# Row vectors turned on TensorE instead of through DRAM, lane sums on VectorE, low parts on GpSimd

## The reference

```python
xn = _layernorm(x, axis=-1)
x = x + attn(xn, ...) + ffn(xn, ...)
# attn
q, gate, k, v = split(xn @ w_qkv.T)            # 16, 16, 4, 4 heads of 128
q, k = _rope(_layernorm(q, ...)), _rope(_layernorm(k, ...))
scores = einsum('bhqd,bhkd->bhqk', q, k) / math.sqrt(D)
scores = where(causal, scores, -inf)
out = einsum('bhqk,bhkd->bhqd', softmax(scores), v)
out = (out * sigmoid(gate)) @ w_o.T
# ffn
top_vals, top_idx = top_k(xn @ w_router, 2);  probs = softmax(top_vals)
y = square(relu(xn @ w_fc[e])) @ w_proj[e]     # of a token's two experts, weighted by probs
```

## Time and profile before

| what | value |
|---|---|
| median of 3 runs (lowest to highest) | 2317.14 us (2312.96 to 2319.57) |
| the profiled execution, its own time | 2312.64 us |
| its span, first to last instruction | 2310.8 us |
| mean granted TensorE clock | 0.853 of full speed |
| busy: PE, DVE, ACT, POOL | 71%, 70%, 54%, 55% |
| bytes moved | 112.09 MB, 49 GB/s in the mean |

### The profile page before, as it was taken

One profiled execution on the slowest core, in us unless ns is written; L12 is line 12 of the kernel. 1 busy time (PEld: TensorE's weight loads), 2 busy tenths in 40 slices (PEclk: granted clock), 3 DMA queues, 4 the chain that ended last, 5 costly groups with the idle time before them and its releaser, 6 DMA issues.

```text
span 2310.8 us, 24049 instructions
## 1 busy us (share of the span) xinstructions
PE 1635.4 (71%) x7139; PEld 1284.1 (56%) x7139; DVE 1625.4 (70%) x2926; ACT 1242.2 (54%) x2409; POOL 1272.1 (55%) x1113
## 2 busy tenths in 40 slices
PE   5676676767767777777765767668767568678676
PEld 3455555555546565655644655556545456566564
DVE  7776677776766666877755666677856558688784
ACT  3445455556545555656644545556654346566565
POOL 6655667775644544555643544545555335556464
PEclk8887788878878888898897888889887879898888
DMA  4312311222342122122113212202212132321101
GB/s 164 97 40 29 48 29 37 49 49 55 46 53 51 35 51 48 28 60 56 48 37 58 51 23 58 44 21 67 47 46 53 37 49 44 69 39 33 37 10 46
DMA packets 130451, 112.09 MB, mean 49 GB/s; under 512 B 73872, under 2 KB 99984, under 8 KB 130128
## 3 DMA queue, kind: packets, MB, share of 16 engines
q1 hardware_dynamic: 126576, 100.29, 21.1%
q0 software_dynamic: 3744, 10.26, 1.6%
HBM read 91.61 MB, written 24.98 MB: 50 GB/s over the span
## 4 chain that ended last, share of the span: by engine, by line
DMA 29%; DVE 10%; PE 5%; issue 3%; POOL 2%; ACT 2%; SPq 0%; POOLq 0%; DVEq 0%; ACTq 0%
DMA inv_of<-row_inv 10%; DMA min_of<-row_min 8%; DMA min_rows<-min_of 4%; DMA inv_rows<-inv_of 3%; DVE pT_lo L1350 2%; PE st_bank L1437 2%; DMA expert_raw<-in_w_proj 2%; DVE t_same L1305 1%; DVE chunk_min L1338 1%; PE bank L1437 1%; DMA y_of<-rows,row_to 1%; POOL lane_sum L942 1%; DVE bank L1335 1%; POOL oT L949 1%; ACT st_bank L1069 1%
## 5 line engine op out<-in xcount | busy, mean ns | idle before, releaser
L942 POOL TENSOR_TENSOR lane_sum<-lane_sum,pT_raw 128x512 f32<-128x512 f32 x420 | 600.7, 1430 | 202.3 <-ACT pT_raw L1079 177.3
L1350 DVE TENSOR_TENSOR pT_lo<-pT_raw,pT_hi 128x512 fp32r<-128x512 f32 x544 | 502.4, 933 | 152.9 <-ACT pT_hi L1086 151.6
L1437 PE MATMUL st_bank<-qT_hi,kT_hi 128*128 128x512 f32 x544 | 262.8, 483 | 341.6 <-ACT st_bank L1069 341.0
L1069 ACT ACTIVATE st_bank<-min_rows 128x512 f32<-128x512 f32 x480 | 284.4, 596 | 322.5 <-DMA min_rows<-min_of 316.4
L1079 ACT ACTIVATE pT_raw<-st_bank 128x512 f32<-128x512 f32 x544 | 322.8, 594 | 191.3 <-PE st_bank L1437 76.7
L1086 ACT ACTIVATE pT_hi<-pT_raw 128x512 fp32r<-128x512 f32 x544 | 338.3, 627 | 60.4 <-PE o_bank L1437 53.6
L1437 PEld LDWEIGHTS st_bank<-qT_hi,kT_hi 128*128 128x128 f32 x544 | 118.2, 217 | 403.4 <-ACT st_bank L1069 388.1
L1437 PE MATMUL o_bank<-pT_hi,v_hi 128*128 128x512 f32 x544 | 240.5, 442 | 65.7 <-DVE pT_lo L1350 57.7
L1338 DVE TENSOR_REDUCE chunk_min<-bank 128x1 f32<-128x512 f32 (+1 forms) x384 | 242.1, 648 | 30.8 <-PE bank L1515 30.5
L949 POOL TENSOR_TENSOR oT<-oT,inv_rows 128x512 f32<-128x512 f32 x63 | 82.9, 1316 | 289.1 <-DMA inv_rows<-inv_of 288.2
L1437 PE MATMUL st_bank<-qT_lo,kT_hi 128*128 128x512 f32 x544 | 241.2, 443 | 0.0
(11 more groups left out here) (176 smaller groups left out, 3779.4 us busy)
## 6 DMA issues: line engine op xcount, KB each, us to landing
min_rows<-min_of SPq DMA_DIRECT2D x64, 256.0 KB, 4.6
inv_rows<-inv_of SPq DMA_DIRECT2D x63, 256.0 KB, 4.8
norm_rows<-kept_tables SPq DMA_DIRECT2D x24, 384.0 KB
made_tables<-kept_tables SPq DMA_DIRECT2D x24, 384.0 KB, 5.2
kept_tables<-made_tables SPq DMA_DIRECT2D x16, 384.0 KB, 3.5
rows<-xs SPq DMA_DIRECT2D x23, 258.0 KB, 3.0
expert_raw<-in_w_fc SPq DMA_DIRECT2D x23, 256.0 KB, 3.4
expert_raw<-in_w_proj SPq DMA_DIRECT2D x23, 256.0 KB, 5.1
```

The source lines that it names most:

```text
L942: pool.tensor_tensor(total, pT_raw[:, (m - 1) % RAW_RING] if j == 1 else total, pT_raw[:, m % RAW_RING], ALU.add).then_inc(summed, 1)
L1069: act.activation(st_bank[m % ST_BANKS][:], masked_min[:] if j == t else min_rows[:, t % 2], ACT.Copy, scale=-1.0)\
L1350: dve.tensor_tensor(pT_lo[:, m % PT_RING], pT_raw[:, m % RAW_RING], pT_hi[:, m % PT_RING].bitcast(F32), ALU.subtract).then_inc(pt_lo_done, 1)
L1437: ins = pe.matmul(out_ap, s, m, start=(start and done == 1), stop=(stop and done == last), skip_group_check=seeded_bank)
```

## The change

The change does six things.

1. **The bound's row vector.** `mu_store` and `mu_load` are gone. PE turns `row_min`, each head's column repeated 128 times along the free dimension, into a bank (MU, four 128x128 transposes per row), and ACT copies the bank to `min_rows` (`mu_take`, 128x512).
2. **The division by the sum.** `inv_store`, `inv_load`, POOL's og and INVB are gone. The gated output is split as it is and projected head by head: OUT is now two banks of two heads, 256 columns each, with as many matmuls as before. In `out_add` DVE multiplies each head's 256 columns by `row_inv`, which lies on the query's own partition there, and adds them to `acc`: four SCALAR_TENSOR_TENSOR of 128x256 per row in place of one TENSOR_TENSOR of 128x256.
3. **Lane sums.** The sums over a row's tiles go from POOL to DVE. They stand in a PSUM bank of their own (`lane_bank`), and only the row's last add writes to `lane_sum` in SBUF, which has one buffer instead of two.
4. **Low parts.** `pT_lo` goes from DVE to POOL, 544 instructions of 128x512.
5. **Rings and banks.** The rings of `pT_raw`, `pT_hi` and `pT_lo` have 4 buffers instead of 3, and 4 banks instead of 5 go round.
6. **The order.** BEGIN and DUE have other numbers, so every engine's instructions are interleaved anew. The last row is no longer an exception.

The core of the diff:

```diff
@@ -51,10 +51,10 @@
-NBANK = 5
+NBANK = 4
 ST_BANKS = 2
-RAW_RING = 3
-PT_RING = 3
+RAW_RING = 4
...
-            "LT": "route", "RANK": "pos", "SUMT": "sums", "INVB": "og"}
+            "LT": "route", "RANK": "pos", "MU": "mu_take", "SUMT": "inv"}
...
-BEGIN = [27.9, 35.95, 43.42, 54.03, 67.6, 78.14, 95.84, 113.51, 135.83, 157.85, 183.65, 208.62, 236.43, 261.23,
...
+BEGIN = [28.22, 35.98, 38.21, 53.97, 63.66, 76.73, 99.25, 107.7, 130.95, 153.01, 183.22, 204.83, 229.02, 266.48,
...
-            add("sp mu", ("mu_store", g, t), 0.45, [mu], last - 20, 2)
-            add("sp mu", ("mu_load", g, t), 0.45, [("mu_store", g, t), old(t2, "seed", t2[1]) if t2 else None], last - 20, 256)
-            add("pool mask", ("masked", g, t), 1.27, [("mu_load", g, t), old(t1, "seed", t1[1]) if t1 else None],
+            add("pe MU", ("MU", g, t), 0.44, [mu], last + DUE["mu"])
+            add("act mu", ("mu_take", g, t), 0.48, [("MU", g, t), old(t2, "masked")], last + DUE["mu"])
+            add("pool mask", ("masked", g, t), 1.27, [("mu_take", g, t), old(t1, "seed", t1[1]) if t1 else None],
...
                 freed = [back("p_lo", RAW_RING)]
                 if m >= RAW_RING:
                     g0, t0, j0 = every[m - RAW_RING]
                     freed.append(("psum", g0, t0, 1 if t0 and not j0 else j0))
-                add("act S", ("exp", g, t, j), 0.5, [("st", g, t, j)] + freed, at + DUE["exp"])
-                add("act PT", ("p_hi", g, t, j), 0.5, [("exp", g, t, j), back("pv", PT_RING)], at + DUE["p_hi"])
-                add("dve PT", ("p_lo", g, t, j), 0.6, [("p_hi", g, t, j)], at + DUE["p_lo"])
+                add("act S", ("exp", g, t, j), 0.48, [("st", g, t, j)] + freed, at + DUE["exp"])
+                add("act PT", ("p_hi", g, t, j), 0.52, [("exp", g, t, j), back("pv", PT_RING)], at + DUE["p_hi"])
+                add("pool PT", ("p_lo", g, t, j), 1.3, [("p_hi", g, t, j)], at + DUE["p_lo"])
                 if j or not t:
-                    add("pool sum", ("psum", g, t, j), 1.27, [("exp", g, t, j), old(t2, "SUMT") if t2 and j < 2 else None],
+                    add("dve sum", ("psum", g, t, j), 0.64, [("exp", g, t, j), old(t1, "SUMT") if t1 and j == t else None],
                         at + DUE["psum"])
                 add("pe PV", ("pv", g, t, j), 0.695, [("p_lo", g, t, j), ("v_lo", g, t), old(t1, "og0") if t1 and not j else None],
                     at + DUE["pv"])
 
-            add("pe SUMT", ("SUMT", g, t), 0.43, [("psum", g, t, t)], after + DUE["sumt"])
-            add("dve sums", ("sums", g, t), 0.85, [("SUMT", g, t), old(t2, "inv_store")], after + DUE["sumt"])
+            add("pe SUMT", ("SUMT", g, t), 0.44, [("psum", g, t, t)], after + DUE["sumt"])
+            add("dve inv", ("inv", g, t), 0.85, [("SUMT", g, t), old(t2, "out_add", HG // 2 - 1)], after + DUE["sumt"])
             add("dve og0", ("og0", g, t), 0.6, [("pv", g, t, t), ("tanh", g, t // QUAD, HG - 1), old(t2, "og_lo")],
                 after + DUE["og0"])
-            if (g, t) == LAST_TILE:
...
-            else:
-                add("sp inv", ("inv_store", g, t), 0.45, [("sums", g, t)], after - 20, 2)
-                add("sp inv", ("inv_load", g, t), 0.45, [("inv_store", g, t), old(t2, "og")], after - 20, 256)
-                add("pool og", ("og", g, t), 1.27, [("og0", g, t), ("inv_load", g, t)], after + DUE["og"])
-                add("act og", ("og_hi", g, t), 0.52, [("og", g, t), old(t1, "OUT")], after + DUE["og"])
-                add("dve og", ("og_lo", g, t), 0.6, [("og_hi", g, t)], after + DUE["og"])
-                add("pe OUT", ("OUT", g, t), 1.44, [("og_lo", g, t), ("wo_lo", g)], after + DUE["out"])
-                add("dve out", ("out_add", g, t), 0.34, [("OUT", g, t)], after + DUE["out_add"])
+            add("act og", ("og_hi", g, t), 0.52, [("og0", g, t), old(t1, "OUT", HG // 2 - 1)], after + DUE["og"])
+            add("dve og", ("og_lo", g, t), 0.6, [("og_hi", g, t)], after + DUE["og"])
+            for p in range(HG // 2):
+                add("pe OUT", ("OUT", g, t, p), 0.72, [("og_lo", g, t), ("wo_lo", g)], after + DUE["out"])
+                add("dve out", ("out_add", g, t, p), 0.72, [("OUT", g, t, p), ("inv", g, t)], after + DUE["out_add"])
...
+        lane_bank = ctx.enter_context(nc.psum_tensor("lane_bank", [P, CHUNK], F32))
...
+                elif kind == "p_lo":
+                    m = tile_number[a]
+                    w.wait_ge(pt_hi_done, m + 1)
+                    pool.tensor_tensor(pT_lo[:, m % PT_RING], pT_raw[:, m % RAW_RING], pT_hi[:, m % PT_RING].bitcast(F32),
+                                       ALU.subtract).then_inc(pt_lo_done, 1)
...
+                elif kind == "mu_take":
+                    g, t = a
+                    n = g * T + t
+                    w.wait_ge(filled, fill["MU", g, t])
+                    if n >= 2:
+
+                        g2, t2 = tile_before(g, t, 2)
+                        w.wait_ge(masked_done, n - 1)
+                        w.wait_ge(seeded, tile_number[g2, t2, t2] + 1)
+                    act.activation(min_rows[:, t % 2], bank("MU", g, t)[:], ACT.Copy).then_inc(mu_taken, 1)
...
+                elif kind == "psum":
+                    g, t, j = a
+                    n, m = g * T + t, tile_number[g, t, j]
+                    total = lane_sum if j == t else lane_bank
+                    w.wait_ge(exp_done, m + 1)
+                    w.wait_ge(wg_lo_done, 2)
+                    if j == t and n:
+
+                        w.wait_ge(filled, fill["SUMT", *tile_before(g, t)])
+                    w.wait_ge(summed, number[step] - 1)
+                    if t == 0:
+                        dve.tensor_copy(total[:], pT_raw[:, m % RAW_RING]).then_inc(summed, 1)
+                    else:
+                        dve.tensor_tensor(total[:], pT_raw[:, (m - 1) % RAW_RING] if j == 1 else lane_bank[:], pT_raw[:, m % RAW_RING],
+                                          ALU.add).then_inc(summed, 1)
...
+                    if n >= 2:
+
+                        g2, t2 = tile_before(g, t, 2)
+                        w.wait_ge(acc_done, acc_number["out_add", g2, t2, HG // 2 - 1])
...
-                elif kind == "out_add":
-                    g, t = a
-                    w.wait_ge(filled, fill["OUT", g, t])
-                    if (g, t) == LAST_TILE:
-                        w.wait_ge(last_out, 1)
+                    w.wait_ge(filled, fill["OUT", g, t, p])
+                    w.wait_ge(inv_done, g * T + t + 1)
                     w.wait_ge(acc_done, acc_before[step])
-                    dve.tensor_tensor(acc[:, t, :], bank("OUT", g, t)[:, 0:C], acc[:, t, :], ALU.add)\
-                        .then_inc(acc_done, 1)
+                    for i in range(2):
+                        h = 2 * p + i
+                        dve.scalar_tensor_tensor(acc[:, t, :], bank("OUT", g, t, p)[:, i * C:(i + 1) * C], row_inv[:, t % 2, h:h + 1],
+                                                 acc[:, t, :], ALU.mult, ALU.add).then_inc(acc_done, 1)
+                        w.wait_ge(acc_done, acc_number[step] - 1 + i)
                 elif kind == "fc_lo":
...
+                elif kind == "MU":
+                    g, t = a
+                    count = len(chunks_of(t))
+                    if count > 1:
+                        w.wait_ge(min_done, number["min", g, t])
+                    else:
+                        w.wait_ge(chunk_min_done, number["max", g, t, HG - 1, 0])
+                    for h in range(HG):
+                        ins = pe.transpose(bank("MU", g, t)[:, h * P:(h + 1) * P], row_min[:, t % 2, h:h + 1].to_broadcast([P, P]),
+                                           ident_f[:])
+                    ins.then_inc(filled, 1)
                 elif kind == "SUMT":
                     g, t = a
                     w.wait_ge(summed, number["psum", g, t, t])
                     for h in range(HG):
-                        ins = pe.transpose(bank("SUMT", g, t)[:, h * P:(h + 1) * P], lane_sum[:, t % 2, h * P:(h + 1) * P], ident_f[:])
-                    ins.then_inc(filled, 1)
...
+                        ins = pe.transpose(bank("SUMT", g, t)[:, h * P:(h + 1) * P], lane_sum[:, h * P:(h + 1) * P], ident_f[:])
                     ins.then_inc(filled, 1)
                 elif kind == "OUT":
-                    g, t = a
+                    g, t, p = a
                     w.wait_ge(og_lo_done, g * T + t + 1)
                     w.wait_ge(wo_lo_done, g + 1)
-                    heads = range(HG) if (g, t) != LAST_TILE else range(HG // 2)
-                    three(bank("OUT", g, t)[:, 0:C], [(ogT_hi[:, h * P:(h + 1) * P], ogT_lo[:, h * P:(h + 1) * P]) for h in heads],
-                          [(wo_hi[:, h, :], wo_lo[:, h, :]) for h in heads], stop=(g, t) != LAST_TILE).then_inc(filled, 1)
...
+                    for i in range(2):
+                        h = 2 * p + i
+                        rows_of = slice(h * P, (h + 1) * P)
```

(3 more changed lines are left out.)

178 lines of the change are left out of this document (44 added, 134 removed), and 10 rows, old and new, of the table BEGIN.

## The result

The changed kernel takes 1835.28 us in the median of four runs (1830.96 to 1836.27) where the kernel before takes 2315.05 on the same chip: a ratio of 0.7923, with a 95% interval of 0.7903 to 0.7942, 20.8% less.

What follows compares the result with a forecast made beforehand. No engine was taken as full: PE's idle 675.4 us came from waits behind two DMA trips. 2310.8 - 394.8 + 47.1 + 25 + 20 - 42 + 40 = 2006 us span, 2012 median, range 1860 to 2155.

Steps and rivals of the forecast that it cites:

- The trips go: PE's waits for ACT's seeds (row_min, first trip) and ogT_lo (row_inv, second trip) return: 341.0 + 53.8 = 394.8 us.
- MU, INVB: On PE, MU's four transposes a row add 47.1 us; dropping INVB saves under 1 us.
- the copy on ACT: 64 copies, 38.1 us, ahead of seeds; at 0.66 us of PE per us of ACT: +25 us.
- low parts on POOL: pT_lo takes longer on POOL than on DVE, partly exposed before pv on PE: +20 us, bounds 0 and 245.
- other waits: Idle time of PE that comes in place of the trips: +40 us, from 0 to +170.
- The clock: PE's clock rises from 0.85 to 0.87, shrinking 1682 us of PE work by 42 us; bounds 0 and 145.
- the five stretches: Five 50 us stretches of the old profile where nearly no seed waited: clock mean 0.87, PE idle 22.8%.
- DVE: DVE's busy time falls by 67 us to about 1558 us, 78% of some 2000; nothing booked for its load.
- Rival 3: POOL's low parts become what pv on PE waits for: slower, about 2500 us; chance 0.05.
- Rival 1: Only the first trip (row_min) pays, the second was late for other reasons: 2119, with low parts 2140 us; chance 0.20.
- Rival 4: Nothing changes: the rotation's chain of a new row takes the trips' place, 2310 us; chance 0.02.
- Rival 2: More comes back: PE's clock at 0.93 as in one stretch, about 1900 us; chance 0.15.

Runs made afterwards that it cites:

- mu_only: Kernel before with only the row_min trip (first trip) replaced by four PE transposes and an ACT copy: ratio 0.9172 to the kernel before.
- inv_only: Kernel before with only the row_inv trip (second trip) gone, the division moved behind the projection: ratio 0.9294 to the kernel before.
- warm: Kernel before with 4 banks and ten filler matmuls ahead of each row's first score tile from the ninth row on: ratio 1.0186 to the kernel before.
- bank4: Kernel before with 4 round banks instead of 5, no filler matmuls, order written anew: ratio 1.0162 to the kernel before.
- min_trip: Changed kernel with row_min sent through DRAM again (mu_store, mu_load): ratio 0.9090 to the kernel before.
- both_trips: Kernel before with both trips replaced; lane sums, low parts, rings, banks and tables as before: ratio 0.8100 to the kernel before.
- swap_back: Changed kernel with lane sums back on POOL in SBUF and pT_lo back on DVE: ratio 0.8260 to the kernel before.
- light_sums: Changed kernel with the lane sums' middle adds on 8 of 512 columns (incomplete computation), same order: ratio 0.7540 to the kernel before.
- warm_after: Changed kernel with six filler matmuls ahead of each row's q transposes from the second group on, same order: ratio 0.7865 to the kernel before.
- rope3: Changed kernel with the rotation's last step as three DVE instructions instead of five, same order: ratio 0.7896 to the kernel before.
- rope_cost: Changed kernel with the planner told 5.5 us instead of 2.2 us for the rotation's step: ratio 0.8605 to the kernel before.
- landing: Kernel before, both trips kept, planner told 9.1 us for the stores and 4.6 us for the repeating loads: ratio 0.8814 to the kernel before.

## Why the prediction was right, and where it was wrong

The mechanism was right: the trips' waits are the bulk of the gain. Two terms of the sum were mis-sized, the clock (-42 us, measured -144) and the idle time that comes in place of the trips (+85 us, measured +14).

**The trips go: right.** Booked -394.8 us of PE's waits; PE's idle time fell by 381.2. No DMA is left in the seeds' waits, and MU with its copy stands where 13.7 us stood. Both waits themselves, 341.0 and 53.8 us, are 7.6 and 4.2 us now. The sum is right for both trips together only: alone they brought 8.3 and 7.1%, together 19.0%.

**MU, INVB: right.** MU took 39.6 us for 47.1 booked.

**What comes in place: mis-sized.** +25 (the copy on ACT), +20 (low parts on POOL) and +40 (other waits) were booked as idle time of PE, 85 us. PE's idle time says 394.8 - 381.2 = 14 us. The copy's 38.9 us lie in ACT's idle time: PE waits 7.6 us for seeds, so the rate of 0.66 us of PE per us of ACT, taken from an ACT that stood before a DMA, did not hold for work on an ACT that is free. PE waited 3.2 us for low parts (its weight loads 9.0), not 20. A new wait of the booked kind did come, 180.4 us for the rotated row and so 127 more than before, but PE's other waits fell by almost as much, 125 us: for `pT_lo` from 57.7 to 3.2, for the experts' `rows` from 42.7 to nothing, for `feat_lo` from 21.3 to 3.8. That they would fall was booked at nothing. A slip in the sum stands behind the +40 too: it says that the terms so far leave PE idle for 14%, but 280.6 + 25 + 20 us of 1966 are 16.6%. The band that it then gives, 14 to 23%, did hold: PE's idle share is 16.0%. The sum already stood there before the 40 us were added. The 84% of busy PE among the signs is not the sum's either: 1640 of 2006 us are 82%; that 84.0% was measured is luck.

**The clock: mis-sized, the largest miss.** Booked at 0.87, -42 us, with -145 as its bound at 0.93 (from the 0.85 of the rows; from 0.853, as the profile gives it, -37 and -139). The clock came out at 0.93: booked PE work without the clock term was 1682.5 us, measured 1538.8, which is -144. The step that failed is the mean of the five stretches, 0.87, as forecast of a program without the trips. They were free of the first trip's waits alone; those of the second still stood in them. The runs bear this out: with the first trip alone gone (mu_only) the clock is 0.883, near those stretches, with the second alone gone (inv_only) 0.880, and with both gone 0.923. How a wait pulls the clock down, the timeline of PE in the kernel before shows (start us, us, line, operation, count, idle before):

```profile
1112.52 0.40 PE L1437 MATMUL o_bank<-pT_lo,v_hi 128*128 128x512 f32 x1
1112.75 0.39 PE L1437 MATMUL o_bank<-pT_hi,v_lo 128*128 128x512 f32 x1
...
1120.67 0.80 PE L1437 MATMUL st_bank<-qT_hi,kT_hi 128*128 128x512 f32 x1 [6.02 <-ACT st_bank L1069]
1121.26 0.63 PE L1437 MATMUL st_bank<-qT_lo,kT_hi 128*128 128x512 f32 x1
1121.69 0.63 PE L1437 MATMUL st_bank<-qT_hi,kT_lo 128*128 128x512 f32 x1
...
1125.17 0.40 PE L1437 MATMUL o_bank<-pT_hi,v_lo 128*128 128x512 f32 x1
1125.40 0.39 PE L1437 MATMUL st_bank<-qT_hi,kT_hi 128*128 128x512 f32 x1
1125.63 0.40 PE L1437 MATMUL st_bank<-qT_lo,kT_hi 128*128 128x512 f32 x1
```

Before the wait, matmuls of one size start 0.23 us apart, behind it 0.43 us apart, and from 1124 us on 0.23 again: the two levels of the clock, 2.4 and 1.2 GHz. This gap cost its own length and then about 3 us of matmuls at half speed. So the trips' waits had a second price, which belonged into their term. warm against bank4 shows it as cause (clock 0.83 to 0.86 by filled gaps alone), though the time did not follow there, as the trips still stood. PE's busy and idle time add up to the span, so in PE's account the clock makes 102 of the 173 us by which the span fell short of the 2006 booked (1833.0), and the 85 - 14 = 71 us of the point above are the rest. It is an account, not a cause for each us: no run shows the kernel after at a clock of 0.87.

**DVE: wrong.** Forecast 1558 us, measured 1676.9. The new instructions were right: lane sums 253.5 + 51.5 + 38.4 + 3.3 = 346.7 us and one copy group, booked 347; `acc` 122.8, booked 115. The surplus is in instructions that the change does not touch: L1245 265.2 us for 163.6, L1241 96.3 for 78.0, and `ogT_lo`, with two operands in SBUF, at 1131 ns for 1026. The shared port was weighed in the prediction for the lane sums, where it held; the step that failed is to have left all other DVE instructions at the price of the kernel before. The booked sum itself was good: with one trip put back (min_trip) the same 3055 instructions took 1561.6 us, 605 and 581 ns for the rotation's. Nor do denser engines alone do it: without the low parts on POOL the rotation's took 690 and 709 ns (both_trips) and 672 and 698 (swap_back). 851 and 958 ns came only where both trips were gone and POOL had the low parts. It did not refute the time, since 1558 and 1677 both lie below the span, but light_sums shows that DVE's load bounds what is left.

**Rival 3 (POOL before pv): refuted**, 3.2 and 9.0 us. **Rival 1** is what mu_only measured: 0.917, 2125 us by the kernel before's 2317, where it had 2119 and 2140. What it denied, that the second trip pays once the first is gone, is 0.8100 / 0.9172, another 11.7%. **Rival 4** did not occur: the rotation's chain lay close, but cost PE 127 us more than before, not 341. **Rival 2** named the clock of 0.93, on one stretch of five, and was given 0.15; it booked the same 85 us of waits and so still came out 65 us too high.

**Open.** That an instruction of the rotation waits for POOL is read from the times at which it ends; no run here moved one of its operands into PSUM, for which no bank is free, or took POOL's work away from beside it. Why the swap pays even in the kernel before is open, and for every run with a new order, how much of its difference the order makes. How far an order with true costs for all steps would come was not tried either. No complete kernel here is told apart from the changed one as faster: on its chip warm_after has 0.7865 and rope3 0.7896 against 0.7893 for the changed kernel, with intervals that overlap.

## What to carry to other kernels

A wait of several microseconds on TensorE costs its length and a slow clock behind it. When several such waits are to go, don't take the clock from stretches in which some of them still stand, and expect two trips that fill each other's gaps to bring more together than the product of their parts. When an engine beside VectorE works in SBUF, a small VectorE instruction with two SBUF operands has no price of its own: here it took about 0.35 us or ended with GpSimd's, and its mean rose from 0.61 and 0.52 us to 0.85 and 0.96 when both trips were gone and GpSimd made the low parts. What helped VectorE here was a PSUM operand and less work; merging instructions did not, and moving work to GpSimd paid only in exchange for work with a PSUM operand. Before a DMA trip is built away, give the planner its landing time from the trace: that alone brought over half of the gain here. But one true number among others can also make the order worse, as rope_cost did.

## What the runs showed that was not expected

- The store of 512 single numbers (2 KB) took 9.1 us to land. With both trips gone, `expert_raw` from `w_proj` lands in 2.7 us instead of 5.1; the trips as such are not the cause, since in landing, which keeps them, it is 3.1.
- One PSUM bank less, of five that rotate, and the order that goes with it cost 1.6% (0.9 to 2.3%, bank4).
- Five 128x128 instructions of VectorE took from 1.40 to 6.78 us in the same kernel; the longest single one took 5.7 us, with a median of 350 ns. It is the one shown above beside a scatter issue and four low parts of POOL:

```profile
L1245 DVE SCALAR_TENSOR_TENSOR t_same<-t_same,rstd,norm_rows x120: 337/350/5723, 473.7 to 1713.7; 128x128 f32<-128x128 f32 x120
```
